# Softmax sums in four chunks, and the order of the dispatch rounds' PSUM bank pairs, in an attention + soft-MoE kernel

## The chip, the cores and the metric

One core of one Trainium2 chip runs the whole program. The metric is the device time of one execution in microseconds (us), lower is better. Engines: PE (TensorE matmuls; its weight loads are listed as PEld), DVE (VectorE), ACT (ScalarE), POOL (GpSimd), SP (SyncE, which issues the DMAs). They run side by side, each in its own program order, and wait for one another through counting semaphores.

## The reference

2048 rows of x (32 x 64, width 256) go through a cross attention (32 heads of width 8) and then through a soft mixture of 16 experts with 128 slots each. The change is in the second layer only. Cut to it:

```python
x_ln = layernorm(x) * gamma + beta
logits = einsum('bnd,des->bnes', l2norm(x_ln) * scale, l2norm(mu, axis=0))
dispatch = softmax(logits, axis=1)                       # over the 64 rows of a batch
combine = softmax(logits.reshape(B, N, E * S), axis=-1)  # over the 2048 slots
slot_in = einsum('bnd,bnes->besd', x_ln, dispatch)
h = gelu(einsum('besd,edh->besh', slot_in, W1) + b1)
slot_out = einsum('besh,ehd->besd', h, W2) + b2
out = x + einsum('bsd,bns->bnd', slot_out.reshape(B, E * S, D), combine)
```

Both softmaxes use the same exponentials. Combine needs their sum over the 2048 slots of a row, and per expert (for b2).

## The kernel before

The rows are cut into 16 tiles of 128 (two batches each). A first half of the program does the attention for all tiles; the second, from about 238 us of the span, does the experts, one tile per step, steps 0 to 15. Each engine's order of work is written out by hand. In step s, PE does:

- `dispatch(s)`: six rounds over groups of three experts (the last has one). A round is 12 weight loads and 12 matmul instructions in the trace (4 in the last round): exponentials `eb` of tile s times `xw` (tile s's first-layer products, a column of ones and an identity), L1158. The result of round i lies in a pair of PSUM banks, `HB[i % 3]` and the next. Before, the pairs are 6-7, 4-5, 0-1, so rounds 0 and 3 use 6-7, rounds 1 and 4 use 4-5, rounds 2 and 5 use 0-1. From round 3 on, a round waits until `hidden` has read the pair's earlier content (`hn_ready`).
- `slot_logits(s+1)`: the next tile's logits in four banks (2, 3, 0, 1), L935 to L937, 24 matmuls; before the third it waits for all six rounds' `hn_ready`.
- `combine(s)` (L1165, L1173; banks 5, 6, 7), `expand(s+1)` (banks 2 and 3), `transpose_xl(s+2)` (bank 1, L1117), and `contract(s)` (bank 4; L1179 and 24 matmuls of 256 columns).

ACT does in step s: `eT_copy` (L562, one copy per dispatch round, the transposed exponentials), the gelus (L568), the four exponentials of tile s+1 (`slot_exps`, L554, four chunks of 512 columns, each counted in `e_ready`), `gT_high` (L573), and a sum of squares (L547). A load of a function table stands before the gelus and one before the exponentials.

DVE does in step s: a small `clamp`; `hidden` (per round a reciprocal L853 and a product L855, the normalised hidden values, which waits for that round's `eT_copy`); `center(s+2)` (L809); `gT_low` (a copy of the transposed sums `esT`, L861, then two differences, L865); `xw_copy(s+1)` (L830, twice); `xlT_copy(s+2)` (L821, L823); `sums(s+1)` (one reduction of all 2048 exponentials per row to 16 sums, L837, then five tiny instructions L839 to L845); and `finish(s)` (L872), which waits for `contract(s)`, reads bank 4, writes the output tile and counts `yo_ready`. Round 1 of `dispatch(s+1)` waits for this `yo_ready`, as its pair holds bank 4.

In the rows, `w_raw` is the storage of `xw` and of the output tile, `mu_raw` that of the transposed exponentials and of constants, and `pb` that of the hidden values. Two pieces of order matter:

```python
def finish(t, p):
    dve.wait_ge(y_filled, t + 1)
    dve.wait_ge(rs_step, t * 2 + 2)
```

Before step 0, DVE does `sums(0)` after the last attention tile but one, and ahead of `normalise(15)`.

Of the kernel before, what the change touches and what calls it, by code (L numbers as in the profile page):

```python
# [18 lines left out]
AX = mybir.AxisListType  # L19
# [19 lines left out]
def wait(eng, sem, value):  # L39

    if isinstance(value, int) and value <= 0:
        return
    eng.wait_ge(sem, value)


def build(nc, x, ctx_in, pos, Wq, Wkv, Wout, bout, gamma, beta, mu, scale, W1, b1, W2, b2, out):
    ctx = ExitStack()
    with ctx:
        def sb(name, *shape, dt=F32):
            return ctx.enter_context(nc.sbuf_tensor(name, list(shape), dt))  # L50
# [5 lines left out]
        def sem(name):  # L56
            return ctx.enter_context(nc.semaphore(name))
# [56 lines left out]
        eb = sb("eb", P, EXPERTS, SLOTS)  # L114
        es = sb("es", P, EXPERTS)
# [88 lines left out]
        xlT_ready = sem("xlT_ready")  # L204
        l_filled = sem("l_filled")
        e_ready = sem("e_ready")
# [4 lines left out]
        es_ready = sem("es_ready")  # L211
# [33 lines left out]
        NB = (6, 7, 5, 6)  # L245
        LB = (2, 3, 0, 1)

        HB = (6, 4, 0)

        def flat(t):  # L250

# [21 lines left out]
        def pair(i, n):  # L273

            b0 = HB[i % 3]
            return psum[:, b0:b0 + 2, 0:n * XC].rearrange("p b (n c) -> p b n c", c=XC)
# [189 lines left out]
        def _(act):  # L466
# [81 lines left out]

            def slot_exps(t, p):
                act.wait_ge(rn_ready, t + 1)  # L550
                wait(act, es_ready, t)
                for c in range(4):
                    act.wait_ge(l_filled, t * 4 + c + 1)
                    a.activation(eb[:, 4 * c:4 * c + 4, :].rearrange("p a b -> p (a b)"), bank[LB[c]][:], ACT.Exp,  # L554
                                 scale=rn[:, p:p + 1], bias=nshift[:]).then_inc(e_ready, 1)
# [20 lines left out]
            def ffn_step(s, p, last=False, sums=True):  # L576
                eT_copy(s)
                gelus(s)
                if not last:
                    slot_exps(s + 1, 1 - p)  # L580
                gT_high(s)
                if sums:
                    sumsq(s + 2, p)
# [4 lines left out]
            for gr in range(2):  # L588
                pT_copy(TILES - 1, gr)
            slot_exps(0, 0)  # L590
            for gr in range(2, 4):
                pT_copy(TILES - 1, gr)
# [9 lines left out]
        def _(dve):  # L602
            v = nc.vector
# [105 lines left out]
            def normalise(t):  # L709
                dve.wait_ge(o_filled, t + 1)  # L710
                v.reciprocal(rc[:], bank[4][:, DIM:2 * DIM]).then_inc(rc_done, 1)  # L711
                dve.wait_ge(rc_done, t + 1)
                v.tensor_tensor(oT[:], bank[4][:, 0:DIM], rc[:], ALU.mult).then_inc(oT_ready, 1)
# [92 lines left out]
            def center(t, p):  # L806

                wait(dve, xlT_filled, t - 1)
                v.tensor_scalar(xl[:, p, :], xa[:, t, :], ln2[:, 4, t].unsqueeze(1), ln2[:, 6, t].unsqueeze(1),  # L809
                                ALU.subtract, ALU.mult).then_inc(z_ready, 1)  # L810

            def clamp(t, p):

                dve.wait_ge(ss_ready, t + 1)
                wait(dve, rn_ready, t - 1)
                v.tensor_scalar(sm2[:, p, 0:1], ss[:, p:p + 1], L2_EPS * L2_EPS, None, ALU.max)\  # L816
                    .then_inc(ss_clamped, 1)

            def xlT_copy(t):
                dve.wait_ge(xlT_filled, t + 1)  # L820
                v.tensor_copy(flat(xlT[0]), bank[1][:, 0:DIM]).then_inc(xlT_split, 1)  # L821
                dve.wait_ge(xlT_split, t + 1)
                v.tensor_tensor(flat(xlT[1]), bank[1][:, 0:DIM], flat(xlT[0]).bitcast(F32), ALU.subtract)\  # L823
                    .then_inc(xlT_ready, 1)

            def xw_copy(t):

                for c in range(2):
                    dve.wait_ge(xw_filled, t * 2 + c + 1)
                    v.tensor_tensor(xw[:, 8 * c:8 * c + 8, 0:HID], bank[2 + c].rearrange("p (e h) -> p e h", h=HID),  # L830
                                    b1b[:, 8 * c:8 * c + 8, :], ALU.add).then_inc(xw_ready, 1)

            def sums(t, p):

                wait(dve, esT_filled, t)
                dve.wait_ge(e_ready, t * 4 + 4)
                v.reduce_sum(es[:], eb[:], AX.X).then_inc(es_ready, 1)  # L837
                dve.wait_ge(es_ready, t + 1)
                v.tensor_copy(es3[:, 0, :], es[:]).then_inc(es_high, 1)  # L839
                v.tensor_copy(es3[:, 2, :], es[:]).then_inc(es_split, 1)  # L840
                v.reduce_sum(rs[:, p, 0:1], es[:], AX.X).then_inc(rs_step, 1)
                dve.wait_ge(es_high, t + 1)
                v.tensor_tensor(es3[:, 1, :], es[:], es3[:, 0, :].bitcast(F32), ALU.subtract).then_inc(es_split, 1)
                dve.wait_ge(rs_step, t * 2 + 1)
                v.reciprocal(rs[:, p, 1:2], rs[:, p, 0:1]).then_inc(rs_step, 1)  # L845

            def hidden(t):

                for i, gr in enumerate(HG):
                    n, e0 = len(gr), gr[0]  # L850
                    dve.wait_ge(eT_ready, t * len(HG) + i + 1)
                    src = pair(i, n)
                    v.reciprocal(rh[:, :, e0:e0 + n], src[:, :, :, HID]).then_inc(rh_done, 1)  # L853
                    dve.wait_ge(rh_done, t * len(HG) + i + 1)
                    v.tensor_tensor(hb[:, e0:e0 + n].rearrange("p n b h -> p b n h"), src[:, :, :, 0:HID],  # L855
                                    rh[:, :, e0:e0 + n].unsqueeze(3).broadcast_to([P, 2, n, HID]),
                                    ALU.mult).then_inc(hn_ready, 1)

            def gT_low(t):
                dve.wait_ge(esT_filled, t + 1)  # L860
                v.tensor_copy(esT[:], bank[5][:, 0:P]).then_inc(esT_ready, 1)  # L861
                for c in range(2):
                    high, low = (h[:, 4 * c:4 * c + 4, :].rearrange("p a b -> p (a b)") for h in gT)
                    dve.wait_ge(gT_split, t * 2 + c + 1)
                    v.tensor_tensor(low, bank[6 + c][:], high.bitcast(F32), ALU.subtract).then_inc(gT_ready, 1)  # L865
# [4 lines that stand above are left out]
                if not isinstance(t, int) or t >= 2:  # L870
                    dve.wait_ge(stored[p], (t - p) * 8)
                v.scalar_tensor_tensor(out=yo[:, p, :], in0=bank[4][:, 0:DIM], scalar=rs[:, p, 1:2], in1=xa[:, t, :],  # L872
                                       op0=ALU.mult, op1=ALU.add).then_inc(yo_ready, 1)

            def ffn_step(s, p, last=False, ahead=True):
                if not last:
                    clamp(s + 1, 1 - p)
                hidden(s)
                if ahead:
                    center(s + 2, p)  # L880
                gT_low(s)
                if not last:
                    xw_copy(s + 1)
                if ahead:
                    xlT_copy(s + 2)
                if not last:
                    sums(s + 1, 1 - p)
                finish(s, p)


# [17 lines left out]
            v.tensor_tensor(b2s[2 * EXPERTS:3 * EXPERTS, :], b2_raw[2 * EXPERTS:3 * EXPERTS, :],  # L908
                            b2s[2 * EXPERTS:3 * EXPERTS, :].bitcast(F32), ALU.subtract).then_inc(b2_ready, 1)
            dve.wait_ge(xw_const, 3)  # L910
            sums(0, 0)
            normalise(TILES - 1)
            residual(TILES - 1)
# [15 lines left out]
        def _(pe):  # L929
# [211 lines left out]
            def dispatch(t, last, first=False):  # L1141

                pe.wait_ge(xw_ready, t * 2 + 2)
                for i, gr in enumerate(HG):
                    if i == 1:
                        wait(pe, yo_ready, t)
                        if first:
                            pe.wait_ge(x1_ready, TILES)
                    if i == 2:
                        pe.wait_ge(e_ready, t * 4 + 4)  # L1150
                        if not last:
                            pe.wait_ge(xlT_ready, t + 2)
                    if i >= 3:
                        pe.wait_ge(hn_ready, t * len(HG) + i - 2)
                    for n, e in enumerate(gr):
                        for b in range(2):
                            rows = slice(64 * b, 64 * b + 64)
                            m = mm(bank[HB[i % 3] + b][:, n * XC:(n + 1) * XC], eb[rows, e, :], xw[rows, e, :],  # L1158
                                   start=True, stop=True)
                    m.then_inc(h_filled, 1)  # L1160
# [89 lines left out]
```

## Time and profile before

| | |
|---|---|
| median of 3 runs | 569.67 us (569.51 to 570.97) |
| profiled execution | 568.76 us, of which the span 566.4 us |
| PE busy | 490.9 us, 87% |
| PE weight loads busy | 391.0 us, 69% |
| DVE busy | 387.0 us, 68% |
| ACT busy | 304.8 us, 54% |
| mean granted TensorE clock | 0.946 |

The span runs from the first to the last instruction; the 2.36 us between it and the execution's time lie around it. Busy shares are averages over two halves with different limits. Durations of matmuls are pipelined (they overlap), so the distance between starts is what one costs. A row with xN merges N instructions that follow each other. An idle time in brackets names what ended it. Tensor names are printed without buffer numbers.

### The profile page before, as it was taken

To read this page: it belongs to the slowest core of one execution; us is meant where nothing else is said; L and a number is where in the kernel's file an instruction comes from. 1 tells how busy PE (TensorE), PEld (TensorE's weight loads), DVE (VectorE), ACT (ScalarE), POOL (GpSimd) and SP (SyncE) were. 2 spreads that over 40 slices of the span, in tenths; PEclk is the share of its full clock that TensorE was granted. 3 is DMA by queue.
4 is the path that set the end of the run, shared out by engine and by line. 5 is a ranking of instruction groups with operands and counts; after the bars stand their busy time and mean duration, and the time that the engine had idled before them with its cause. 6 is when DMAs were issued, how large, how long until landed. Compare 5 with 4: busy or idle time off the path is not lost.

```text
span 566.4 us, 14818 instructions
## 1 busy us (share of the span) xinstructions
PE 490.9 (87%) x5784; PEld 391.0 (69%) x5784; DVE 387.0 (68%) x813; ACT 304.8 (54%) x599; POOL 149.0 (26%) x248
## 2 busy tenths in 40 slices
PE   0676999986888788888999999999999999999995
PEld 0454666654656556567887888788878788887885
DVE  5888998977798979945754664475457446654662
ACT  1354656654364635635468446745764575468443
POOL 4339211509282822212112211211121122112100
PEclk9768999999697969997999999999999999999997
DMA  7400000006000200000000000000000000000000
GB/s 198 183 6 6 8 7 6 8 1 159 6 6 5 64 0 1 2 2 1 10 1 11 11 10 0 9 9 9 0 9 9 0 9 9 9 0 9 10 10 10
DMA packets 15730, 11.70 MB, mean 21 GB/s; under 512 B 7072, under 2 KB 15184, under 8 KB 15440
## 3 DMA queue, kind: packets, MB, share of 16 engines
q1 hardware_dynamic: 15696, 11.21, 6.7%
q8 instruction: 26, 0.43, 0.3%
q14 instruction: 8, 0.07, 0.0%
HBM read 9.11 MB, written 2.10 MB: 20 GB/s over the span
## 4 chain that ended last, share of the span: by engine, by line
PE 59%; DVE 28%; ACT 5%; issue 5%; SPq 1%; DMA 1%; POOL 0%; DVEq 0%; ACTq 0%
PE psum L935 11%; PE psum L937 9%; PE psum L936 9%; DVE es L837 6%; PE psum L1158 6%; PE psum L1173 6%; PE psum L985 4%; PE psum L1000 4%; DVE qkr L681 4%; PE psum L1014 3%; DVE rc L711 3%; PE psum L1034 2%; DVE mx L694 2%; DVE pb L699 2%; DVE pb L855 2%
## 5 line engine op out<-in xcount | busy, mean ns | idle before, releaser
L562 ACT COPY mu_raw<-psum 128x384 f32<-128x384 f32 x96 | 41.1, 444 | 131.9 <-PE psum L1158 131.8
L1158 PE MATMUL psum<-w_raw,eb 64*128 64x129 f32 x1024 | 72.2, 287 | 14.7 <-DVE w_raw L872 11.7
L1158 PEld LDWEIGHTS psum<-w_raw,eb 64*128 64x128 f32 x1024 | 63.2, 192 | 23.1 <-DVE w_raw L872 14.7
L477 ACT ACTIVATE pb<-pb 128x512 f32<-128x512 f32 x64 | 39.4, 632 | 66.4 <-DVE pb L699 66.4
L347 POOL TENSOR_TENSOR sm<-sm,mhalf 128x1 f32<-128x1 f32 x16 | 8.8, 549 | 182.6 <-DVE sm L816 182.6
L935 PE MATMUL psum<-mun_h,xlT_l 128*128 128x512 f32 x128 | 52.3, 408 | 0.2 <-DVE xlT_l L823 0.2
L1000 PE MATMUL psum<-ident,pb 128*128 128x128 f32 x256 | 47.1, 315 | 5.9 <-ACT vb L494 3.8
L1000 PEld LDWEIGHTS psum<-ident,pb 128*128 128x128 f32 x256 | 31.9, 159 | 29.0 <-issue 24.6
L855 DVE TENSOR_TENSOR pb<-psum,rh 128x384 f32<-128x384 f32 x96 | 49.2, 513 | 3.3
L936 PE MATMUL psum<-mun_l,xlT_h 128*128 128x512 f32 x128 | 50.6, 395 | 0.0
L937 PE MATMUL psum<-mun_h,xlT_h 128*128 128x512 f32 x128 | 50.6, 395 | 0.0
L694 DVE TENSOR_REDUCE mx<-psum 128x8 f32<-128x512 f32 x64 | 41.0, 682 | 11.9 <-PE psum L985 11.9
L985 PE MATMUL psum<-kT,qT 32*64 32x256 f32 x512 | 46.8, 456 | 0.0
L865 DVE TENSOR_TENSOR gT_l<-psum,gT_h 128x512 fp32r<-128x512 f32 x32 | 20.7, 686 | 38.1 <-ACT gT_h L573 38.1
L554 ACT ACTIVATE eb<-psum,nshift,rn 128x512 f32<-128x512 f32 x64 | 44.9, 776 | 3.3 <-PE psum L937 1.6
L861 DVE CAST esT<-psum 128x128 fp32r<-128x128 f32 x16 | 4.7, 291 | 61.3 <-PE psum L1165 61.3
L481 ACT COPY pT<-psum 128x512 f32<-128x512 f32 x64 | 35.8, 592 | 9.7 <-PE psum L1000 9.6
L699 DVE TENSOR_TENSOR pb<-psum,mx 128x512 f32<-128x512 f32 x64 | 40.9, 679 | 0.0
L1173 PEld LDWEIGHTS psum<-mu_raw,pb 128*64 128x64 f32 x1024 | 32.7, 143 | 6.0 <-issue 4.3
L837 DVE TENSOR_REDUCE es<-eb 128x16 f32<-128x2048 f32 x16 | 36.4, 2276 | 0.0
L936 PE MATMUL psum<-w_l,gT_h 128*128 128x256 f32 x128 | 36.3, 283 | 0.0
L1173 PE MATMUL psum<-mu_raw,pb 128*64 128x64 f32 x1024 | 35.0, 229 | 1.4 <-ACT pb L568 1.4
(160 smaller groups left out, 1163.4 us busy)
## 6 DMA issues: line engine op xcount, KB each, us to landing
mu_raw<-in_L_ffn_mu SPq DMA_DIRECT2D x1, 2048.0 KB, 12.2
out<-w_raw SPq DMA_DIRECT2D x16, 128.0 KB, 1.7
xa<-in_x SPq DMA_DIRECT2D x1, 1536.0 KB, 8.5
ctile<-in_ctx SPq DMA_DIRECT2D x16, 64.0 KB, 1.8
w_raw<-in_L_ffn_W SPq DMA_DIRECT2D x2, 512.0 KB, 5.3
w_raw<-in_L_ffn_W SPq DMA_DIRECT2D x1, 1024.0 KB, 9.3
xa<-in_x SPq DMA_DIRECT2D x1, 512.0 KB, 3.7
mu_raw<-in_L_ffn_b SPq DMA_DIRECT2D x1, 512.0 KB, 3.2
```

Source lines behind the costliest of these rows:

```text
L554: a.activation(eb[:, 4 * c:4 * c + 4, :].rearrange("p a b -> p (a b)"), bank[LB[c]][:], ACT.Exp, scale=rn[:, p:p + 1], bias=nshift[:]).the ...
L694: v.reduce_max(mx[:, gr, :], bank[gr][:].rearrange("p (h k) -> p h k", k=SEQ), AX.X)\
L699: v.tensor_tensor(pb[:, p, gr], bank[gr][:].rearrange("p (h k) -> p h k", k=SEQ), mx[:, gr, :].unsqueeze(2).broadcast_to([P, 8, SEQ]), ALU ...
L837: v.reduce_sum(es[:], eb[:], AX.X).then_inc(es_ready, 1)
L855: v.tensor_tensor(hb[:, e0:e0 + n].rearrange("p n b h -> p b n h"), src[:, :, :, 0:HID], rh[:, :, e0:e0 + n].unsqueeze(3).broadcast_to([P, ...
L935: mm(o, a[1], b[0], start=first, stop=False)
L936: mm(o, a[0], b[1], start=False, stop=False)
L937: return mm(o, a[0], b[0], start=False, stop=last)
L985: m = mm(bank[g][cols, 256 * half:256 * half + 256].rearrange("p (j n) -> p j n", j=4), qT[rows, half, cols], kT[rows, half, :, cols], sta ...
L1000: m = nc.tensor.transpose(bank[6 + gr % 2][:, i * P:(i + 1) * P], pb[:, p, gr, 2 * i:2 * i + 2, :].rearrange("p h k -> p (h k)"), ident[:])
L1158: m = mm(bank[HB[i % 3] + b][:, n * XC:(n + 1) * XC], eb[rows, e, :], xw[rows, e, :], start=True, stop=True)
L1173: m = mm(bank[6 + c][64 * r:64 * r + 64, i * P + b * 64:i * P + b * 64 + 64], hb[:, e, b, :], eT[:, e, b * 64:b * 64 + 64], start=True, st ...
```

## The change

- The reduction over 2048 exponentials becomes `slot_sums`: four reductions of 512, each after its own chunk's `e_ready`, and each writes four of the 16 sums. They stand after `center` and ahead of the copy of `esT`.
- The copy of `esT` becomes a function of its own, in the same place ahead of `gT_low`.
- The small rest of `sums` moves from behind `xlT_copy` to between `xw_copy` and `xlT_copy`; `es_ready` counts four per tile, and ACT's wait follows.
- The bank pairs become 6-7, 0-1, 4-5. So round 1 has banks 0-1 and waits for tile s's four exponentials and for `xlT_copy(s+1)`; round 2 has banks 4-5 and waits for `yo_ready`. The waits of PE swap places accordingly.

```diff
@@ -245,7 +245,7 @@
         NB = (6, 7, 5, 6)
         LB = (2, 3, 0, 1)
 
-        HB = (6, 4, 0)
+        HB = (6, 0, 4)
 
         def flat(t):
 
@@ -548,7 +548,7 @@
 
             def slot_exps(t, p):
                 act.wait_ge(rn_ready, t + 1)
-                wait(act, es_ready, t)
+                wait(act, es_ready, t * 4)
                 for c in range(4):
                     act.wait_ge(l_filled, t * 4 + c + 1)
                     a.activation(eb[:, 4 * c:4 * c + 4, :].rearrange("p a b -> p (a b)"), bank[LB[c]][:], ACT.Exp,
@@ -830,12 +830,16 @@
                     v.tensor_tensor(xw[:, 8 * c:8 * c + 8, 0:HID], bank[2 + c].rearrange("p (e h) -> p e h", h=HID),
                                     b1b[:, 8 * c:8 * c + 8, :], ALU.add).then_inc(xw_ready, 1)
 
+            def slot_sums(t):
+
+                for c in range(4):
+                    dve.wait_ge(e_ready, t * 4 + c + 1)
+                    v.reduce_sum(es[:, 4 * c:4 * c + 4], eb[:, 4 * c:4 * c + 4, :], AX.X).then_inc(es_ready, 1)
+
             def sums(t, p):
 
                 wait(dve, esT_filled, t)
-                dve.wait_ge(e_ready, t * 4 + 4)
-                v.reduce_sum(es[:], eb[:], AX.X).then_inc(es_ready, 1)
-                dve.wait_ge(es_ready, t + 1)
+                dve.wait_ge(es_ready, t * 4 + 4)
                 v.tensor_copy(es3[:, 0, :], es[:]).then_inc(es_high, 1)
                 v.tensor_copy(es3[:, 2, :], es[:]).then_inc(es_split, 1)
                 v.reduce_sum(rs[:, p, 0:1], es[:], AX.X).then_inc(rs_step, 1)
@@ -856,9 +860,11 @@
                                     rh[:, :, e0:e0 + n].unsqueeze(3).broadcast_to([P, 2, n, HID]),
                                     ALU.mult).then_inc(hn_ready, 1)
 
-            def gT_low(t):
+            def esT_copy(t):
                 dve.wait_ge(esT_filled, t + 1)
                 v.tensor_copy(esT[:], bank[5][:, 0:P]).then_inc(esT_ready, 1)
+
+            def gT_low(t):
                 for c in range(2):
                     high, low = (h[:, 4 * c:4 * c + 4, :].rearrange("p a b -> p (a b)") for h in gT)
                     dve.wait_ge(gT_split, t * 2 + c + 1)
@@ -878,13 +884,15 @@
                 hidden(s)
                 if ahead:
                     center(s + 2, p)
+                if not last:
+                    slot_sums(s + 1)
+                esT_copy(s)
                 gT_low(s)
                 if not last:
                     xw_copy(s + 1)
+                    sums(s + 1, 1 - p)
                 if ahead:
                     xlT_copy(s + 2)
-                if not last:
-                    sums(s + 1, 1 - p)
                 finish(s, p)
 
 
@@ -908,6 +916,7 @@
             v.tensor_tensor(b2s[2 * EXPERTS:3 * EXPERTS, :], b2_raw[2 * EXPERTS:3 * EXPERTS, :],
                             b2s[2 * EXPERTS:3 * EXPERTS, :].bitcast(F32), ALU.subtract).then_inc(b2_ready, 1)
             dve.wait_ge(xw_const, 3)
+            slot_sums(0)
             sums(0, 0)
             normalise(TILES - 1)
             residual(TILES - 1)
@@ -1143,13 +1152,13 @@
                 pe.wait_ge(xw_ready, t * 2 + 2)
                 for i, gr in enumerate(HG):
                     if i == 1:
+                        pe.wait_ge(e_ready, t * 4 + 4)
+                        if not last:
+                            pe.wait_ge(xlT_ready, t + 2)
+                    if i == 2:
                         wait(pe, yo_ready, t)
                         if first:
                             pe.wait_ge(x1_ready, TILES)
-                    if i == 2:
-                        pe.wait_ge(e_ready, t * 4 + 4)
-                        if not last:
-                            pe.wait_ge(xlT_ready, t + 2)
                     if i >= 3:
                         pe.wait_ge(hn_ready, t * len(HG) + i - 2)
                     for n, e in enumerate(gr):
```

## Rows read from the trace of the kernel before

**Rows 1.** The page: chain that ended last, share of the span by line.
```profile
PE psum L935 11%; PE psum L937 9%; PE psum L936 9%; DVE es L837 6%; PE psum L1158 6%; PE psum L1173 6%; PE psum L985 4%; PE psum L1000 4%; DVE qkr L681 4%; PE psum L1014 3%; DVE rc L711 3%; PE psum L1034 2%; DVE mx L694 2%; DVE pb L699 2%; DVE pb L855 2%
```

**Rows 2.** Windows: busy us of PE, PEld, DVE, ACT, POOL, granted clock, DMA share, GB/s.
```profile
420.00:460.00 40.00, 38.17 (x391) 32.63 (x390) 22.43 (x56) 24.10 (x41) 7.45 (x20) 1.00 0.02 7
...
555.00:559.00 4.00, 3.36 (x62) 3.36 (x64) 0.69 (x1) 1.69 (x3) 0.00 (x0) 0.50 0.00 0
```

**Rows 3.** Waits, 330 to 566 us: total us, times, longest.
```profile
PEld psum L1158 <- DVE w_raw L872: 11.9, 12, 1.1
```

**Rows 4.** The chain in order of time, one step: start us, us, what.
```profile
449.60 2.29 DVE es L837
...
452.48 0.50 DVE w_raw L872
...
453.02 0.96 PE psum L1158 x12
...
454.01 0.49 ACT mu_raw L562
...
454.75 0.57 DVE pb L855
...
455.36 1.19 PE psum L1158 x16
```

**Rows 5.** Timeline of the same step, its dispatch: start us, us, engine, line.
```profile
451.05 0.28 PE L937 MATMUL psum<-w_h,gT_h 128*128 128x256 f32 x1
451.26 0.75 PEld L1158 LDWEIGHTS psum<-w_raw,eb 64*128 64x128 f32 x12
...
452.24 0.48 ACT L562 COPY mu_raw<-psum 128x384 f32<-128x384 f32 x1 [5.67 <-PE psum L1158]
...
453.40 0.56 DVE L855 TENSOR_TENSOR pb<-psum,rh 128x384 f32<-128x384 f32 x1
...
455.44 0.56 DVE L855 TENSOR_TENSOR pb<-psum,rh 128x384 f32<-128x384 f32 x1
...
456.48 0.19 PEld L935 LDWEIGHTS psum<-mun_h,xlT_l 128*128 128x128 f32 x1
```

**Rows 6.** The end of the kernel, from the chain in order of time.
```profile
563.43 0.13 PE psum L937
...
563.59 0.48 DVE w_raw L872
```

**Rows 7.** Timeline of step 1's dispatch, 277 to 282 us.
```profile
277.34 0.75 PEld L1158 LDWEIGHTS psum<-w_raw,eb 64*128 64x128 f32 x12
...
278.44 0.48 DVE L872 SCALAR_TENSOR_TENSOR w_raw<-psum,rs,xa 128x256 f32<-128x256 f32 x1
...
280.22 0.56 DVE L855 TENSOR_TENSOR pb<-psum,rh 128x384 f32<-128x384 f32 x1
...
281.61 0.56 DVE L855 TENSOR_TENSOR pb<-psum,rh 128x384 f32<-128x384 f32 x1
```

**Rows 8.** Timeline of the last step's dispatch (step 15), DVE.
```profile
549.36 0.56 DVE L855 TENSOR_TENSOR pb<-psum,rh 128x384 f32<-128x384 f32 x1
...
551.15 0.56 DVE L855 TENSOR_TENSOR pb<-psum,rh 128x384 f32<-128x384 f32 x1
```

**Rows 9.** The page, costliest groups: the row reduction of 128x512.
```profile
L694 DVE TENSOR_REDUCE mx<-psum 128x8 f32<-128x512 f32 x64 | 41.0, 682 | 11.9 <-PE psum L985 11.9
```

**Rows 10.** The chain in order of time: two such reductions back to back.
```profile
231.44 1.20 DVE mx L694 x2
```

**Rows 11.** Timeline of DVE at the start of the second half.
```profile
248.51 2.29 DVE L837 TENSOR_REDUCE es<-eb 128x16 f32<-128x2048 f32 x1
```

**Rows 12.** Timeline of the stretch ahead of it, 442 to 449 us.
```profile
442.42 2.78 ACT L554 ACTIVATE eb<-psum,nshift,rn 128x512 f32<-128x512 f32 x4
...
445.71 1.29 DVE L865 TENSOR_TENSOR gT_l<-psum,gT_h 128x512 fp32r<-128x512 f32 x2 [2.23 <-ACT gT_h L573]
...
448.14 0.37 PE L1179 MATMUL psum<-b2s,esT 128*128 128x256 f32 x1
```


## The prediction

> **What bounds the kernel now.** I first read the page's chain that ended last, by line. The matmuls lead it, but one DVE row stands high, the reduction L837 with 6% of the span [rows 1]: some 34 us, which is all of its 16 executions of about 2.28 us. DVE is no bottleneck by its busy share, so this reduction is on the path through its place in the order. Next I read the windows and the clock: in the second half PE is busy 38.17 us in each 40 at a granted clock of 1.00, its upper level of 2.4 GHz [rows 2]. So about 1 us per step of idle time is visible, and a little more where modelled matmul ends cover the gap. The waits say what it is: PE's weight loads for the dispatch rounds wait 11.9 us for L872, `finish`, in 12 steps [rows 3].
>
> The chain in order of time gives the mechanism [rows 4]. The big reduction runs 449.60 to 451.89, the tiny ones follow, `finish` starts at 452.48, and round 1 can start only at 453.02. Round 1's `eT_copy` (454.01), its product on DVE (454.75) and then round 4 (455.36, which reuses round 1's banks) all hang on this. The timeline shows what `finish` really needs: the last matmul of `contract` started at 451.05 and ends at 451.33 [rows 5]. At the kernel's very end, where DVE had nothing else to do, `finish` started 0.03 us after the modelled end of that matmul [rows 6]. So here `finish` is about 1.1 us late, and only because DVE is in the reduction.
>
> The ruler for one step is the start of round 0's weight loads, 451.26; call it T. Twelve loads take 0.75 us with the last one's own length of some 0.16, so the next round could start at about T+0.65; it starts at T+1.76. Round 0's copy on ACT starts at T+0.98 (452.24). DVE's products start at 453.40 for round 0 (T+2.14) and 455.44 for round 2 (T+4.18). The slot logits start at 456.48, which is 1.04 after round 2's product, since round 5 waits for that product [rows 5].
>
> **Part 1: the reduction leaves the place ahead of `finish`.** Before, DVE came to the reduction at 449.60, with the second `xw_copy` and `xlT_copy` done. The tiny sums, 451.89 to 452.48, add 0.6 us, so without the reduction DVE is free at about 450.2 [rows 4]. The contraction ends at 451.33. `finish` starts at about 451.36 and ends, with its 0.50, at 451.86, which is T+0.60. Round 1 was due at T+0.65. So this part alone takes the stall away, and the new place of the banks hardly adds to it.
>
> What is late next is the chain through ACT and DVE. Round 0's copy ends at 452.72 (T+1.46). The product follows the copy's end by the reciprocal: in round 1 the copy starts at 454.01 and the product at 454.75, 0.74 later [rows 4]. So round 0's product starts at T+0.98+0.74 = T+1.72. From there the products come at DVE's own pitch. In step 1 they stood back to back: 280.22 and 281.61 are rounds 0 and 2, 1.39 for two, 0.70 each [rows 7]. The copies come early enough for that (round 1's at about T+0.65+0.99, done by T+2.12, and DVE wants it at T+2.2). So round 2's product starts at T+1.72+1.39 = T+3.11, and the slot logits at T+4.15, against T+5.22 now. **Gain 1.07 us in each full step.** Rounds 3 and 4 wait for rounds 0 and 1 by a few tenths, which is inside this number.
>
> There are 13 such full steps (2 to 14), 13.9 us. Step 1 has a block of small moments on DVE between `finish` and `hidden`: its first product stands 1.78 behind the start of `finish` (278.44, 280.22). With `finish` at 277.44, 0.10 after round 0 at 277.34, as in a full step, the gain is that of `finish`, 1.0 us [rows 7]. In the last step `finish` was less late (no `xlT_copy`): products of rounds 0 and 2 start at 549.36 and 551.15, 1.79 apart; at the pitch it would be 1.39, so 0.4 us [rows 8]. Step 0 has no `finish` ahead of it: nothing.
>
> **Part 2: four chunks in place of one.** No row shows a 512-column sum out of SBUF. The nearest is the maximum over 128x512, 682 ns alone [rows 9], and two in 1.20 us, a pitch of 0.60 [rows 10], both out of PSUM. The floor is a quarter of the whole, 0.57 [rows 11]; the top is 0.68 with no overlap. I take 0.60. In a full step this lies in idle time: the four exponentials run 442.42 to 445.20 at 0.67 us each, so each sum runs under the next exponential, and only the last is exposed: it starts at about 445.24 and hands on at 445.84. Queued behind it are the copy of `esT` (0.2) and the two differences, which started at 445.71 and now start at about 446.1, so 0.35 to 0.4 late [rows 12]. Who waits for them is the contraction: it starts at 448.14 and needs the first difference, done at about 446.75, and the `esT` copy. Both have over 1 us of room. All of this moves with PE, since ACT's chain of copies, gelus and exponentials hangs on the rounds' copies, which come 1.07 earlier too. Even if ACT's chain did not move, the first difference at 446.75 would still be ahead of 448.14 - 1.07 = 447.07. Cost in a full step: zero. Cover gone, it would be 0.4.
>
> At the start of the half it is exposed: the exponentials of tile 0 are long done, the reduction runs at 248.51 on the path to `normalise(15)` [rows 11], and four chunks cost 3 x 0.60 + 0.68 = 2.48 against 2.29. **Loss 0.2 us, once** (bounds 0 and 0.45).
>
> A rule speaks against this part. The Trainium skill, "VectorE: DVE Perf Modes", section on the TRN2 errata, says that an instruction reading SBUF pays a fixed latency, once for a large tile and once per tile for many small ones; "Perfetto Trace Analysis", section Optimizing Scalar/DVE Operations, puts it at about 60 ns per DVE instruction on SBUF. Estimated by that page, the start would lose 0.18 us, and 2.9 us of DVE time over 16 tiles would be hidden; the trace's pitch above gives 0.12 to 0.2 us for the four, so it agrees.
>
> **Part 3: the banks.** Round 1 now waits for four exponentials of tile s (done 6 us before) and for `xlT_copy(s+1)`. The latter ends at about 450.2 in the new order; round 1 is due at 451.91. It costs nothing with 1.7 us of room, and one or more if DVE ran late by more. Round 2's wait for `yo_ready` is over at T+0.6, and it is due at T+1.3. Rounds 4 and 5 swap pairs; the third slot logits wait for all six products either way: the last product, at the pitch, is done at about T+5.8, and the third logits are due at T+4.15+2.8. Zero. What part 3 brings is insurance: were `finish` up to 0.65 late, round 1 would not notice.
>
> **The sum.** 13.9 + 1.0 + 0.4 - 0.2 = 15.1 us. From the profiled execution of 568.76: 553.7. That execution lies 0.91 under the median shown, so the forecast is 569.67 - 15.1 = **554.6 us**, a step period of 18.2 instead of 19.3.
>
> **Rivals.**
> - *`finish` stays late, and only the banks help* (6%). If the tiny sums or a wait I did not see keep `finish` at 452.48, `hidden` still starts at 453.40 and only the pitch improves: round 2's product at 454.79 in place of 455.44, 0.65 x 13 + 0.4 = 8.9 us, 561 us. For it: the product of round 0 already stands 0.92 behind the start of `finish`. Against: nothing on DVE is left to hold it.
> - *All stall goes* (4%). 60 loads at 0.054 bring round 5 to T+3.3 and the logits to T+3.7: 1.5 us x 14, some 21 us, 548.5. For it there would have to be earlier products, and the copy of round 0 and the DVE pitch forbid it.
> - *Given back later* (3%). PE reaches the contraction 1.07 earlier and finds `gT` not ready, as DVE's queue is longer. That needs the differences over 1 us later than worked out. Result about 569.
> - *Slower: the chunks hold up the contraction* (2%). The copy of `esT` and the differences now queue behind four sums in DVE's order. With a chunk of x us over 0.67, the first difference is done at about 443.24 + 4x + 0.95. It passes the contraction's start, 448.2, at x = 1.0, and eats the whole gain at x = 1.27 us. At x = 2.28, if the reduction's cost went by instruction, a step would lose 4 us: some 630 us in all. Against it: the same number of columns took 0.68 at most [rows 9].
>
> The forecast itself has 85%. Within it the start and the tail can move by 1 to 2 us: PE stands idle ahead of them, and the clock is at its lower level of 1.2 GHz there (0.50 from 555 to 559 [rows 2]); when it rises depends on work that now comes at other times. Per step, an error of 0.2 us makes 2.8 us.
>
> **Numbers.** Likeliest 554.6, its own range 551.5 to 557.5; the range, which reaches to the banks-only case, is 551.0 to 559.5. No change, here, is within 0.3% (1.7 us), about what measurement of this kernel can tell. Faster: 0.85 + 0.06 + 0.04 = 0.95; same 0.03; slower 0.02.
>
> **What would show it.** Right: PE's wait for L872 gone from the waits; the reductions four per step under the exponentials, 0.6 to 0.7 us; DVE idle ahead of `finish`, released by L937; 18.2 us between two `finish`; products of a step 0.70 apart from the first on; short waits of PE for L855 (rounds 3 to 5). Wrong: waits of L1179 or L935 for `gT_l` or `esT`, or of round 1 for `xlT_l`; a chunk near 1 us; products that still stand 1.3 apart.

## The result, and the profile after

| | before | after |
|---|---|---|
| median | 569.67 us (569.51 to 570.97, 4 runs) | 552.09 us (551.52 to 552.62, 4 runs) |
| profiled execution | 568.76 us | 552.62 us |
| span | 566.4 us | 550.4 us |

The ratio is 0.9686, 95% interval 0.9669 to 0.9704: 17.6 us faster, where 15.1 was forecast. Between the two profiled executions it is 16.1 us. Timed again beside e9 and e10, the same kernel had a ratio of 0.9788 (0.9701 to 0.9874; e8, below), some 12 us; what is the same both times is the length of a step. Medians, here and below, are over all executions, and the ratios leave out those in the slower of two states that this kernel shows.

First the page of the changed kernel, the chain that ended last, by line, then the group of the new reductions:

```profile
PE psum L944 14%; PE psum L945 12%; PE psum L946 12%; PE psum L1167 8%; PE psum L1182 6%; PE psum L994 4%; PE psum L1009 4%; DVE qkr L681 4%; PE psum L1023 4%; DVE rc L711 3%; PE psum L1043 2%; DVE mx L694 2%; DVE pb L699 2%; DVE pb L859 2%; ACT vb L494 2%
...
L837 DVE TENSOR_REDUCE es<-eb 128x4 f32<-128x512 f32 x64 | 42.9, 686 | 61.3 <-ACT eb L554 61.3
```

The reduction L837, 6% of the span in [rows 1], is gone from the chain, though DVE now spends more time in it (42.9 us in place of 36.4). Its 61.3 us of idle time, released by ACT, say that it now waits for the exponentials. Next the waits of the changed kernel from 330 to 550 us (total us, times, longest), against [rows 3]:

```profile
DVE es L837 <- ACT eb L554: 44.8, 11, 4.5
...
DVE w_raw L878 <- PE psum L946: 19.5, 13, 2.4
...
PEld psum L1167 <- DVE pb L859: 3.0, 12, 0.3
```

PE's wait of 11.9 us for `finish` is gone. The wait runs the other way: `finish` (now L878) waits for the contraction, 1.43 us in the step below. So the place of the tiny sums, which moved too and take some 0.5 us, cannot have held it up there; no run moves them by themselves. What is left of stalls in the rounds is 0.25 us per step, for a product of `hidden` (L859). The timeline of a full step shows both (against [rows 5] and [rows 12]):

```profile
423.84 0.28 PE L946 MATMUL psum<-w_h,gT_h 128*128 128x256 f32 x1
...
424.04 2.09 PEld L1167 LDWEIGHTS psum<-w_raw,eb 64*128 64x128 f32 x36
424.36 0.48 DVE L878 SCALAR_TENSOR_TENSOR w_raw<-psum,rs,xa 128x256 f32<-128x256 f32 x1 [1.43 <-PE psum L946]
425.03 0.48 ACT L562 COPY mu_raw<-psum 128x384 f32<-128x384 f32 x1 [5.66 <-PE psum L1167]
425.77 0.56 DVE L859 TENSOR_TENSOR pb<-psum,rh 128x384 f32<-128x384 f32 x1
426.38 1.69 PEld L1167 LDWEIGHTS psum<-w_raw,eb 64*128 64x128 f32 x28 [0.25 <-DVE pb L859]
427.16 0.56 DVE L859 TENSOR_TENSOR pb<-psum,rh 128x384 f32<-128x384 f32 x1
...
428.20 0.19 PEld L944 LDWEIGHTS psum<-mun_h,xlT_l 128*128 128x128 f32 x1
...
433.44 2.79 ACT L554 ACTIVATE eb<-psum,nshift,rn 128x512 f32<-128x512 f32 x4
434.25 2.69 DVE L837 TENSOR_REDUCE es<-eb 128x4 f32<-128x512 f32 x4 [4.07 <-ACT eb L554]
437.06 1.28 DVE L871 TENSOR_TENSOR gT_l<-psum,gT_h 128x512 fp32r<-128x512 f32 x2
439.16 0.37 PE L1188 MATMUL psum<-b2s,esT 128*128 128x256 f32 x1
```

With T = 424.04 (T is again the start of round 0's weight loads), rounds 0 to 2 go out in one stretch of 36 loads; round 0's product starts at T+1.73, round 2's at T+3.12 (worked out: 1.72 and 3.11). The slot logits follow at 428.20, T+4.16 (worked out: 4.15). The four sums (434.25 to 436.94) lie under the exponentials (433.44 to 436.23), and the differences start at 437.06 with 1.4 us left for the first before the contraction wants it.

PE's clock has no part in the gain of a step. It was at 1.00 before [rows 2], and it is in the changed kernel (windows: busy us of PE, PEld, DVE, ACT, POOL, then the granted clock):

```profile
400.00:440.00 40.00, 39.88 (x405) 34.42 (x404) 26.17 (x71) 23.92 (x42) 6.18 (x18) 1.00 0.02 7
```

To tell the gain of a step from the rest, I measure from the transposition of the sums (L1165, L1174) of one step to that of another. All differences are after minus before.

| stretch | before, us | after, us | difference | forecast |
|---|---|---|---|---|
| start of the span to first `xlT_copy` (attention) | 237.89 | 238.43 | +0.5 | 0 |
| from there to step 0's transposition | 31.08 | 31.26 | +0.2 | +0.2 |
| to step 1's | 19.38 | 18.39 | -1.0 | -1.0 |
| to step 14's (13 steps) | 251.14 | 236.96 | -14.2 | -13.9 |
| to the combine of step 15 | 16.15 | 15.76 | -0.4 | -0.4 |
| to the end of the span | 10.76 | 9.60 | -1.2 | 0 |

The sum is -16.0, the difference of the spans. Each full step gains 1.09 us.

### The profile page after: what moved, and what is told of

It is laid out like the page before. It is cut to its first block, busy times and chain, and to the rows that moved or that the text cites. A ratio compares the mean times of both kernels' runs of the same rounds, so it can differ in the third digit from the quotient of the medians.

```text
span 550.4 us, 14914 instructions
## 1 busy us (share of the span) xinstructions
PE 485.2 (88%) x5784; PEld 388.5 (71%) x5784; DVE 390.8 (71%) x861; ACT 305.3 (55%) x599; POOL 148.7 (27%) x248
## 4 chain that ended last, share of the span: by engine, by line
PE 71%; DVE 19%; ACT 5%; issue 3%; SPq 1%; DMA 1%; POOL 0%; DVEq 0%; ACTq 0%
PE psum L944 14%; PE psum L945 12%; PE psum L946 12%; PE psum L1167 8%; PE psum L1182 6%; PE psum L994 4%; PE psum L1009 4%; DVE qkr L681 4%; PE psum L1023 4%; DVE rc L711 3%; PE psum L1043 2%; DVE mx L694 2%; DVE pb L699 2%; DVE pb L859 2%; ACT vb L494 2%
## 5 line engine op out<-in xcount | busy, mean ns | idle before, releaser
L837 DVE TENSOR_REDUCE es<-eb 128x4 f32<-128x512 f32 x64 | 42.9, 686 | 61.3 <-ACT eb L554 61.3
L1167 PE MATMUL psum<-w_raw,eb 64*128 64x129 f32 x1024 | 68.3, 284 | 2.9 <-DVE w_raw L830 1.7
L859 DVE TENSOR_TENSOR pb<-psum,rh 128x384 f32<-128x384 f32 x96 | 49.3, 513 | 3.3
L694 DVE TENSOR_REDUCE mx<-psum 128x8 f32<-128x512 f32 x64 | 41.1, 684 | 11.9 <-PE psum L994 11.9
L944 PE MATMUL psum<-w_h,gT_l 128*128 128x256 f32 x128 | 36.0, 281 | 0.0
L946 PE MATMUL psum<-w_h,gT_h 128*128 128x256 f32 x128 | 35.9, 280 | 0.0
```

The source lines that it names most:

```text
L694: v.reduce_max(mx[:, gr, :], bank[gr][:].rearrange("p (h k) -> p h k", k=SEQ), AX.X)\
L837: v.reduce_sum(es[:, 4 * c:4 * c + 4], eb[:, 4 * c:4 * c + 4, :], AX.X).then_inc(es_ready, 1)
L944: mm(o, a[1], b[0], start=first, stop=False)
L946: return mm(o, a[0], b[0], start=False, stop=last)
```

## The experiments

"Step" is the distance between the starts of `finish` of steps 0 and 13, divided by 13: 19.33 us before, 18.25 after. Single executions of the kernel before spread from 562.6 to 572.4 us on the chips of these experiments; where a few us matter, the step from the trace is the firmer number. The ratios of e1 (0.9774) and e8 (0.9788) show it: they cannot tell the order alone from the whole change.

| kernel | median, us | ratio to before, 95% interval | step, us |
|---|---|---|---|
| e1 order only | 555.32 | 0.9774 (0.9726 to 0.9822) | 18.35 |
| e2 banks only | 557.54 | 0.9808 (0.9749 to 0.9867) | 18.72 |
| e3 chunks only | 571.23 | 1.0058 (1.0022 to 1.0094) | 19.51 |
| e4 whole reduction, moved | 557.27 | 0.9813 (0.9755 to 0.9870) | 18.36 |
| e5 every chunk twice | 566.89 | 0.9976 (0.9937 to 1.0016) | 18.97 |
| e6 first sums earlier | 547.77 | 0.9683 (0.9618 to 0.9747) | 18.25 |
| e7 more of the start earlier | 549.04 | 0.9633 (0.9579 to 0.9686) | 18.25 |
| e8 the changed kernel again | 555.32 | 0.9788 (0.9701 to 0.9874) | 18.25 |
| e9 four bank pairs | 546.87 | 0.9645 (0.9550 to 0.9740) | 17.87 |
| e10 four pairs and e6 | 543.07 | 0.9593 (0.9500 to 0.9686) | 17.87 |

**e1: the order alone.**

```diff
-        HB = (6, 0, 4)
+        HB = (6, 4, 0)
...
                     if i == 1:
+                        wait(pe, yo_ready, t)
...
```

> The changed kernel with the bank pairs and PE's waits of before (6-7, 4-5, 0-1; round 1 waits for yo_ready), so only the sums and their order are changed. In the trace of the changed kernel finish starts 0.31 us behind round 0 (424.05, 424.36), not 0.10 as I had worked out, so it ends at T+0.80 and round 1 of the old pairs, due at T+0.65, would wait some 0.2 us. Theory A (the order gives the gain, the banks next to none): round 2's product comes 0.12 us later per step than in the changed kernel, 1.7 us over 14 steps, so about 553.8 us, and at least 13 of the 16 to 17.6 us are there. Theory B (the banks carry the gain): within 5 us of the kernel before, 565 or more.

Its step is 18.35 us: 0.98 of the 1.08 us are there without the banks, and the banks add 0.10 to that. Theory A stands, B falls. The median, 555.32, lies 1.5 over the number given; by its interval the ratio allows 553.1 to 558.6. The timeline of a step of e1:

```profile
426.99 4.19 PEld L1167 LDWEIGHTS psum<-w_raw,eb 64*128 64x128 f32 x64
...
427.31 0.48 DVE L878 SCALAR_TENSOR_TENSOR w_raw<-psum,rs,xa 128x256 f32<-128x256 f32 x1 [1.43 <-PE psum L946]
427.98 0.48 ACT L562 COPY mu_raw<-psum 128x384 f32<-128x384 f32 x1 [5.66 <-PE psum L1167]
...
428.83 0.48 ACT L562 COPY mu_raw<-psum 128x384 f32<-128x384 f32 x1 [0.37 <-PE psum L1167]
...
430.27 0.56 DVE L859 TENSOR_TENSOR pb<-psum,rh 128x384 f32<-128x384 f32 x1
...
431.30 0.19 PEld L944 LDWEIGHTS psum<-mun_h,xlT_l 128*128 128x128 f32 x1
```

Round 1's copy comes 0.85 behind round 0's, where back to back it is 0.67 (425.03, 425.70 in the changed kernel): this is the 0.2 us for which round 1 waits for `yo_ready`. Round 2's product starts at T+3.28 against T+3.12, and the slot logits at T+4.31 against T+4.16. In the next step of e1 they start at T+4.22, and so on in turn; in the changed kernel it is T+4.15 to T+4.16 in all full steps. The mean of the two differences, 0.11, is what the banks give.

**e2: the banks alone.** The first edit of the diff and the exchange of PE's waits, on the kernel before.

> The kernel before with only the bank pairs and PE's waits changed; the one reduction stays ahead of finish. Theory A: finish stays at T+1.2, hidden starts behind it, round 2's product comes 0.65 us sooner per step (1.39 behind round 0's in place of 2.04): 8.9 us, so about 560.8 us. Theory B: 555 or less. If hidden's start were not what decides: no change, 569.

The step is 18.72 us, 0.61 under before. A step of e2 shows the late `finish` and what the banks buy:

```profile
426.30 2.27 DVE L837 TENSOR_REDUCE es<-eb 128x16 f32<-128x2048 f32 x1
...
427.96 1.42 PEld L1158 LDWEIGHTS psum<-w_raw,eb 64*128 64x128 f32 x24
...
429.25 0.48 DVE L872 SCALAR_TENSOR_TENSOR w_raw<-psum,rs,xa 128x256 f32<-128x256 f32 x1
429.62 0.48 ACT L562 COPY mu_raw<-psum 128x384 f32<-128x384 f32 x1 [0.19 <-PE psum L1158]
429.79 2.64 PEld L1158 LDWEIGHTS psum<-w_raw,eb 64*128 64x128 f32 x40 [0.41 <-DVE w_raw L872]
429.93 0.56 DVE L855 TENSOR_TENSOR pb<-psum,rh 128x384 f32<-128x384 f32 x1
...
431.52 0.56 DVE L855 TENSOR_TENSOR pb<-psum,rh 128x384 f32<-128x384 f32 x1
```

Round 1 runs past `finish` (24 loads in one stretch), and round 2 takes the wait, 0.41 us in place of 1.02. The 0.61 is near the 0.65 expected partly by luck: round 0's product starts at T+1.97 (expected: T+2.14 as before), and round 2's follows 1.59 behind it, not 1.39. The median, 557.54, is 3.3 under the 560.8 expected; in the profiled execution 2.6 of that lie between the last two `finish` (12.76 us against 15.40 before), outside the steps. So either part alone takes more than half of the stall away: 0.98 and 0.61 us, and both together 1.08. They overlap.

**e3: the chunks alone, in the old place.**

```diff
-                v.reduce_sum(es[:], eb[:], AX.X).then_inc(es_ready, 1)
-                dve.wait_ge(es_ready, t + 1)
+                for c in range(4):
+                    v.reduce_sum(es[:, 4 * c:4 * c + 4], eb[:, 4 * c:4 * c + 4, :], AX.X).then_inc(es_ready, 1)
+                dve.wait_ge(es_ready, t * 4 + 4)
```

> The kernel before with the one reduction replaced by four of 512 columns at its old place ahead of finish, all four behind the wait for the last exponential. The four took 2.48 us at the start of the changed kernel against 2.29 for the one, and they lie on the path in every step: 0.18 us x 15 plus 0.2 at the start, some 2.8 us slower than before, about 572.4 us. If chunking by itself had a gain, it would be faster than before.

(ACT's wait for `es_ready` counts by four too.) It costs 0.18 us per step, as expected, and the ratio says 3.3 us slower (1.2 to 5.4). Here cutting by itself only costs; it has to be bought back by the place.

**e4: the whole reduction in the new place.**

```diff
-                for c in range(4):
-                    dve.wait_ge(e_ready, t * 4 + c + 1)
-                    v.reduce_sum(es[:, 4 * c:4 * c + 4], eb[:, 4 * c:4 * c + 4, :], AX.X).then_inc(es_ready, 1)
+                dve.wait_ge(e_ready, t * 4 + 4)
+                v.reduce_sum(es[:], eb[:], AX.X).then_inc(es_ready, 1)
```

> The changed kernel with the one reduction of 2048 columns in place of the four, at the new place; it waits for the last exponential. From the changed kernel's step (exponentials end at 436.23): the reduction ends at about 438.55, the first difference at 439.4, and the contraction wants it at 439.28, so 0.15 us per step is lost there, and finish comes another 0.1 late, which the new pairs hide. Theory A: 2 to 4 us over the changed kernel in all, about 555. Theory C (the chunks under the exponentials are what makes the new place work): more than 0.5 us per step is lost, 560 or more.

(The waits for `es_ready` count by one again.) The step is 18.36 us, 0.11 over the changed kernel. It is lost where it was expected, at the contraction. In e4 the first load of `gT_l` starts 0.27 us behind the load ahead of it:

```profile
423.63 0.19 PEld L1187 LDWEIGHTS psum<-b2s,esT 128*128 128x128 f32 x1
423.90 0.19 PEld L943 LDWEIGHTS psum<-w_h,gT_l 128*128 128x128 f32 x1
```

In the changed kernel it is 0.11 (420.90, 421.01). So the chunks are worth 0.11 us per step, 1.5 us in all, less the 0.2 that they cost at the start. Theory C falls.

**e5: every chunk twice.**

```diff
-                    v.reduce_sum(es[:, 4 * c:4 * c + 4], eb[:, 4 * c:4 * c + 4, :], AX.X).then_inc(es_ready, 1)
+                    for dst in (es_b, es):
+                        v.reduce_sum(dst[:, 4 * c:4 * c + 4], eb[:, 4 * c:4 * c + 4, :], AX.X).then_inc(es_ready, 1)
```

> The changed kernel with every chunk summed twice, first into a spare tile, then into the sums: two instructions of 0.60 us pitch per exponential, 1.2 us against the exponentials' 0.67. It tries the rival for slower. By its arithmetic as I put it down (the contraction is passed at 1.0 us per chunk, 4 us per step for each further us) a step would lose 0.8 us, with 2.4 at the start some 14 us: 566. Worked out anew from the changed kernel's step: the eight end at 439.1, the first difference at 439.87 in place of about 437.8, the contraction wants it at 439.28, so 0.6 us per step, 9 us, and 2.4 at the start: 564. If the room ahead of the contraction were larger than I think: 555.

The step is 18.97 us: 0.72 lost, between the 0.6 and the 0.8. (The waits for `es_ready` count by eight.) The rival for slower is a real mechanism, and its threshold is near where it was put: at 1.2 us per chunk a third of the gain of a step is left. The chunks' starts (pitch 0.59 to 0.60) and the two new waits of PE in the timeline of e5:

```profile
425.53 0.69 DVE L839 TENSOR_REDUCE es_b<-eb 128x4 f32<-128x512 f32 x1 [3.99 <-ACT eb L555]
426.13 0.68 DVE L839 TENSOR_REDUCE es<-eb 128x4 f32<-128x512 f32 x1
...
429.69 0.68 DVE L839 TENSOR_REDUCE es<-eb 128x4 f32<-128x512 f32 x1
...
430.61 0.19 PEld L1190 LDWEIGHTS psum<-b2s,esT 128*128 128x128 f32 x1 [0.19 <-DVE esT L867]
...
431.21 0.18 PEld L946 LDWEIGHTS psum<-w_h,gT_l 128*128 128x128 f32 x1 [0.41 <-DVE gT_l L873]
```

**e6 and e7: the sums of tile 0.** In e6, `slot_sums(0)` stands ahead of `residual(14)`, where DVE is idle; in e7 the preparation of b2 and the tiny sums do too.

```diff
             normalise(TILES - 2)
+            slot_sums(0)
             residual(TILES - 2)
...
-            slot_sums(0)
             sums(0, 0)
```

> The changed kernel with slot_sums(0) moved ahead of residual(14), where DVE sits idle for 5.6 us while PE and ACT make tile 0's logits and exponentials. The 2.48 us of the four sums leave the path at the start of the second half: about 2.4 us less than the changed kernel, 549.7; up to 2 us more if TensorE's clock, which stood at its lower level in dispatch(0), is back sooner. If something else than DVE set that path, the expansion or the project of the last tile: less than 1 us.

> As e6, and the preparation of b2 and the tiny sums of tile 0 moved ahead of residual(14) too, so that normalise(15) comes right behind that residual. Another 1.1 us of DVE work leaves the path, but the attention product of tile 15 ends at about 249.2, so at most 0.6 of it counts: 549.0. Same as e6 if the attention product decides.

From the first `xlT_copy` to dispatch(0) it is 16.76 us in e6 and 16.69 in e7, against 19.69 in the changed kernel and 19.31 before. That is 2.9 and 3.0 us, a little over the 2.4 of the sums; the same work took 19.43 in e8, 20.04 in e1 and 20.05 in e9, so the gain is known to some 0.3 us. `normalise(15)` starts 0.3 earlier in e7 than in e6, and next to nothing of it arrives. In e6 PE's clock stood at 1.00 there and dispatch(0) took 4.40 us in place of 5.93; in e7, whose start is just as short, it took 5.82, with the clock at 0.50 and 0.69 in its first two windows of 2 us. So the faster clock does not come surely with the shorter start. The medians of e6 and e7 (expected 549.7 and 549.0) cannot tell the two apart.

**e8 to e10: what sets the step now.** e9 gives the rounds a fourth pair, banks 2-3, which are idle at that time:

```diff
-        HB = (6, 0, 4)
+        HB = (6, 0, 2, 4)
...
-                    if i == 2:
+                    if i == 3:
                         wait(pe, yo_ready, t)
...
-                    if i >= 3:
-                        pe.wait_ge(hn_ready, t * len(HG) + i - 2)
+                    if i >= 4:
+                        pe.wait_ge(hn_ready, t * len(HG) + i - 3)
...
+                    if c == 0:
+                        wait(pe, hn_ready, t * len(HG) - 3)
```

(and `i % 4` in place of `i % 3`, twice.)

> The changed kernel unaltered, beside e9 and e10 on one chip, as the measure for them: single executions of the kernel before spread from 562.65 to 572.03 us on the chips of e1 to e7, and from 569.5 to 571.0 where the change was timed. Expected: ratio 0.97, a step of 18.25 us as before.

> The changed kernel with a fourth pair of banks for the dispatch rounds, 2-3, which lies idle between xw_copy and the slot logits: pairs 6-7, 0-1, 2-3, 4-5. Rounds 4 and 5 then wait for the products of rounds 0 and 1 in place of 1 and 2, and the first slot logits for round 2's product. In the changed kernel round 5 waits for round 2's product (T+3.11) and the logits start at T+4.15. With four pairs nothing in the six rounds waits: 64 loads at 0.054 us and the turn to the next shape bring the logits to about T+3.65, if the chain copy, product, round is what sets the step now. 0.5 us x 15, 7.5 us under the changed kernel. If PE's loads or the exponentials' chain on ACT set it: less than 0.1 us per step.

> e9 with the first sums moved ahead of residual(14), as in e6. If the two savings lie at different places they add up: 7.5 and, as e6 showed, 2.5 for the sums and 1.5 for the faster dispatch(0), in all some 11 us under the changed kernel, about 541. If the clock at the start is what e6 gained and it comes and goes by itself: only 7.5 and 2.5.

e8 has the step of 18.25 again, but a ratio of 0.9788, not 0.97. Part of the difference is in the attention half: its profiled execution came to the first `xlT_copy` at 243.13 us, with the same instructions that took 238.43 in the first profile. e9's step is 17.87 us, 0.38 under the changed kernel. The 64 loads are one stretch, PE's wait for L859 is in none of its steps any more, and the slot logits start at T+3.78 (timeline and windows of e9; PE's busy time is 40.00 of 40 us, after 39.88 in the changed kernel and 38.17 in [rows 2]):

```profile
422.69 3.65 PEld L1169 LDWEIGHTS psum<-w_raw,eb 64*128 64x128 f32 x64
...
426.47 0.19 PEld L944 LDWEIGHTS psum<-mun_h,xlT_l 128*128 128x128 f32 x1
```

```profile
400.00:440.00 40.00, 40.00 (x416) 35.13 (x415) 26.11 (x73) 22.96 (x40) 6.17 (x18) 1.00 0.02 7
```

I had expected 0.5, with the logits at T+3.65: the loads come at 0.055 us and not 0.054, and the turn to the next shape is a little longer than I took it. The chain of copy, product and next round was what set the changed kernel's step, and without it PE's own work does. e10 adds the earlier sums: 543.07 us (541.76 to 548.1), the fastest version, 2.2% under the changed kernel run beside it. Its dispatch(0) took 5.46 us, with the clock at 0.52 and 0.63 in such windows, and e9's, whose start is not shortened, 5.24; so the clock gain of e6 did not come back. By the medians e9 lies 8.5 us under e8 and e10 12.3 (forecast: 7.5 and 11). The steps account for 5.3 (14 x 0.38) and the start for some 2.7 more; the rest lies in neither, so that these medians come near the forecast is in part luck.

## Why the prediction was right, point by point

- **`finish` is late because of the reduction, and PE's stall is its work: right.** e1 moves only the sums and has 0.98 of the 1.08 us per step.
- **What is late next is copy, reciprocal, product: right.** Products at T+1.73 and T+3.12, against 1.72 and 3.11. e9, which takes the wait for them away, gains 0.38 more.
- **1.07 us per full step: 1.09 measured**, over 13 steps 14.2 in place of 13.9. Step 1: 1.0 and 1.0. Last step: 0.4 and 0.4.
- **`finish` at T+0.10: wrong, without effect on the sum.** It starts at T+0.31 and T+0.22 in turn in the full steps. So round 1 of the old pairs would have waited some 0.2 and 0.1 us (e1), and "the new place of the banks hardly adds" is 0.10 us per step, 1.3 us in all. It was small, as stated, but I had put it at zero.
- **The chunks: right in price, a little low in worth.** Four cost 0.18 us more than one (e3), 0.2 at the start. I took their place under the exponentials as free and did not price a whole reduction in the new place; e4 does, 0.11 us per step.
- **The room ahead of the contraction: right.** Only doubled sums use it up (e5), and the price is 0.72 us per step against the 0.8 of the rival's arithmetic.
- **The prices of two rivals: near.** Banks only: 0.65 us per step, and 0.61 in e2. All stall gone: 1.5 us per step, and 1.46 in e9 (19.33 less 17.87), which needed the fourth pair; the prediction rightly held that the products forbid it with three.
- **The difference of 2.5 us between forecast and median is not in the steps.** 1.2 us are the tail: the combine of the last tile took 2.97 us in place of 3.69, and windows of 2 us show the clock at its lower level, 0.50, up to 560 and in most of the next window before, and at 0.50 in one window only after.

```profile
541.00:543.00 2.00, 2.00 (x54) 2.00 (x52) 0.28 (x1) 0.85 (x2) 0.00 (x0) 0.67 0.00 0
543.00:545.00 2.00, 2.00 (x22) 1.88 (x19) 0.98 (x2) 0.59 (x1) 0.00 (x0) 0.50 0.03 8
545.00:547.00 2.00, 2.00 (x18) 2.00 (x18) 0.12 (x1) 0.00 (x0) 0.00 (x0) 0.97 0.00 0
```

The same stretch in the kernel before:

```profile
556.00:558.00 2.00, 2.00 (x44) 2.00 (x42) 0.00 (x0) 0.44 (x2) 0.00 (x0) 0.50 0.00 0
558.00:560.00 2.00, 2.00 (x29) 1.88 (x26) 0.70 (x2) 0.84 (x2) 0.00 (x0) 0.50 0.03 8
560.00:562.00 2.00, 2.00 (x13) 2.00 (x12) 0.68 (x1) 0.00 (x0) 0.00 (x0) 0.58 0.00 0
```

And in e8, which is the changed kernel again:

```profile
545.00:547.00 2.00, 1.72 (x58) 1.72 (x60) 0.00 (x0) 1.27 (x3) 0.00 (x0) 1.00 0.00 0
547.00:549.00 2.00, 1.84 (x24) 1.57 (x19) 1.38 (x2) 0.66 (x2) 0.00 (x0) 1.00 0.03 8
```

The range had 1 to 2 us for this. Another 1.4 us is that the profiled execution before lay 0.9 under its median and the one after 0.5 over its own. The steps gave 0.3 more than forecast, what lies around the span 0.1, and the attention took 0.5 longer, the other way: 1.2 + 1.4 + 0.3 + 0.1 - 0.5 = 2.5. From `finish` of step 14 to that of step 15 the traces have 15.40 (before), 14.27 (after), 15.42 (e1), 12.76 (e2), 15.35 (e4) and, for the same kernel as after, 13.20 (e8). The length goes with the clock: it stays at 1.00 in e2 and e8, stands at 0.50 for 6 to 7 us before, in e1 and in e4, and for some 3 us after. The changed kernel alone differs by 1.1 us in this from one execution to the other, so the 1.2 us of the tail cannot be put down to the change; that they fell on the good side is luck. Why the clock falls in one execution and not in the other stays open.

## What to carry to other kernels

An instruction off the critical path by its busy share can be on it by its place: ask what is queued behind it on its engine and who waits for that. Two ways to take a stall away (do the late thing sooner, or let the waiter do something else first) overlap, so price each alone and both together. After the stall went, the next limit here was the chain of hand-overs behind it; a fourth buffer that was idle anyway removed it for another 0.38 us per step.

## What the runs showed of the hardware

- `finish` starts 0.31 to 0.32 us behind round 0 (424.05, 424.36) and 0.22 to 0.23 (442.28, 442.50) in turn inside the loop, whose body is two steps, but 0.10 to 0.11 outside it (278.07, 278.17 in step 1; 533.19, 533.30 in step 15). Inside the loop the wait counts depend on the loop's register, and a row of DVE's queue (FUSED_REGOPS, 64 ns) stands at this line in its 12 executions in the loop and in no other. That these account for the further 0.1 to 0.2 us was not tried, and they do not say why every second step has less of it.
- The granted clock of the attention half differs between executions of identical code: 0.83 from 40 to 60 us and 1.00 from 180 to 200 in the first profile of the changed kernel, 0.71 and 0.88 in e8, which reached the first `xlT_copy` 4.7 us later. This spread is larger than several of the effects studied here, so they are read from the step inside one trace.
- Four sums (`reduce_sum`) of 512 columns out of SBUF come at a pitch of 0.59 to 0.60 us, 0.69 alone, much as the maximum out of PSUM in [rows 9, 10].
